# Reordering one stretch of the round in a two-stream transformer layer: where one stream's first scores run

## The chip, the cores and the metric

The kernel runs on one core of one Trainium2 chip. The metric is the device time of one execution in microseconds, taken as the median of several runs. Lower is better.

## What is computed

The first half of the reference is an attention block over eight sequences of 1024 rows of width 256. The second half, which the change concerns, takes that result `x` through two layers of local attention and a gated feed-forward network. Cut to what matters:

```python
h = shift_token(x)                     # second half of the width comes from the row before
q, k, v = split(h @ wqkv, 3)           # 8 heads of 64
q, k = l2norm(q) * qs, l2norm(k) * ks
q, k = rotary_xpos(q, k)
sim = q @ k.T                          # windows of 128 rows against 256 keys, masked
o = softmax(sim) @ v
x = x + o @ wo
h = layernorm(shift_token(x)) * lg + lb
a, g = split(h @ w1 + b1, 2)           # 682 each
x = x + (a * gelu(g)) @ w2 + b2
```

All of it is in float32.

## The kernel before

The eight sequences make two streams, X and Y, of four sequences each. A stream works through its sequences in tiles of 128 rows, and through both layers of a tile before the next tile: 4 sequences x 8 tiles x 2 layers = 64 units for each stream. Unit `n` of X and units `n` and `n-1` of Y share one round, so the rounds run over `n` (the helper `rounds`), and every engine has an order of its own for the steps of a round, written out by hand. A word such as `saX:0` is step `sa` of stream X for unit `n`; `woY:1` is step `wo` of stream Y for unit `n-1`. Each engine issues its steps strictly in the order of its string, and a step begins with waits on semaphores that the steps it depends on have raised. Streams have PSUM banks and buffers of their own (banks 0 to 3 for X, 4 to 7 for Y).

The steps of one unit, with the line in which each is issued and the engine:

- `uT` (TensorE, L792) transposes the input, `uTc` (VectorE, L1307 and L1310) takes it out; `ga`, `gb_`, `gb` (L799) and `v_`, `v` (L808) are the projections to q, k and v. Half `a` is heads 0 to 3, half `b` heads 4 to 7.
- `sqa`, `sqb` (ScalarE, L1001) square, `ssa`, `ssb` (VectorE, L1315) sum; `rk`, `rq` (GpSimd, L1541 and L1545) make the inverse norms. `rs`, `rot`, `ad` (VectorE, L1329, L1323, L1335) are the rotary products and their sum, and `kn` (VectorE, L1341) scales k by its norm.
- `tqa`, `tka`, `tqb`, `tkb` (TensorE, L820) transpose q and k of each half, two transposes a step. `qca`, `kca`, `qcb`, `kcb` (ScalarE, L1008, L1012) take them out; `vc` (ScalarE, L1005) takes v out. `qca` and `qcb` each wait for both transposing steps of their half.
- `sa`, `sb` (TensorE, L830) are the scores of four heads each. `m0`, `m1` (VectorE, L1353, then L1358) add mask and take the row maximum of them; `e0` to `e3` (ScalarE, L1019) are the exponentials of two heads each, `d0` to `d3` (VectorE, L1363, L1366) divide by the sums, `p0` to `p3` (TensorE, L838) transpose, and `pc0` to `pc3` (ScalarE, L1025) take out.
- `o` (TensorE, L847) is the product with v, `oc` (ScalarE, L1029) takes it out, `wo_`, `wo` (TensorE, L856) multiply by `wo`, `u1` (VectorE, L1370) adds the residual.
- `E` (L863, only where a tile has a tile before it in its sequence) and `sh` (L866) shift the rows on TensorE. `bnu`, `bns`, `ag` (VectorE, L1374, L1377, L1381), `rs` on GpSimd (L1549, L1552) and `hl` (VectorE, L1385) are the layer norm. `h` (TensorE, L871) transposes it, and `hT` (ScalarE, L1033) takes it out.
- `w10`, `w11`, `w12` (TensorE, L881) are the gate products, `ge0` to `ge2` (ScalarE, L1041) the gelu, `ac0` to `ac2` (VectorE, L1396) the product of gate and value, `w20` to `w22` (TensorE, L891) the last product, `ub` and `u2` (VectorE, L1389, L1402) the residual, `fin` and `ln` (VectorE, L1300, L1282) the end and the start of a tile.

Waits that the change touches, in the steps' own words:

```python
elif name in ("qca", "qcb"):
    act.wait_ge(w[f"s_t_ps{g}"], n * 2 + 2)
elif name in ("d0", "d1", "d2", "d3"):
    dve.wait_ge(w["s_exp"], n * 4 + m + 1)
elif name == "E":
    if t > 0:
        pe.wait_ge(w["s_pT"], n * 4 + 3)
elif name in ("w20", "w21", "w22"):
    pe.wait_ge(w["s_act"], n * FC + 2 * j + 2)
```

Of the kernel before, what the change touches and what calls it, by code (L numbers as in the profile page):

```python
# [66 lines left out]
def build(nc, x, Wa, ba, We, be, Wi, Wo, Wv, Wout, Wout_sw, head_vec, sgn, wqkv, q_scale, k_scale,  # L67
# [7 lines left out]
    with ctx:  # L75
# [186 lines left out]
        def rounds(order, do):  # L262

            steps = [(step[:-1], int(lag)) for step, lag in (word.split(":") for word in order.split())]
            names = [word.split(":")[0][-1] for word in order.split()]
            for n in range(-1, UNITS + 2):
                for (step, lag), name in zip(steps, names):
                    if 0 <= n - lag < UNITS:
                        do(step, X if name == "X" else Y, n - lag)
# [303 lines left out]
        def _(pe):  # L573
# [207 lines left out]
            def step_pe(name, w, n):  # L781
# [113 lines left out]
                else:  # L895
# [2 lines left out]
            pe.wait_ge(s_wf, 16 * loads[1])  # L898
            pe.wait_ge(s_zero, 5)
            rounds(("w10X:1 tqaY:1 w11X:1 tkaY:1 w12X:1 saY:1 w20X:1 tqbY:1 w21X:1 tkbY:1 w22X:1 uTX:0 sbY:1 gaX:0 p0Y:1 gb_X:0 "  # L900
                    "p1Y:1 gbX:0 v_X:0 p2Y:1 vX:0 p3Y:1 tqaX:0 tkaX:0 oY:1 saX:0 wo_Y:1 woY:1 tqbX:0 EY:1 shY:1 tkbX:0 sbX:0 hY:1 "
                    "p0X:0 w10Y:1 p1X:0 w11Y:1 p2X:0 w12Y:1 EX:0 w20Y:1 p3X:0 w21Y:1 oX:0 w22Y:1 wo_X:0 uTY:0 woX:0 gb_Y:0 shX:0 "
                    "gbY:0 gaY:0 hX:0 v_Y:0 vY:0"), step_pe)


# [1 line left out]
        def _(act):  # L907
# [87 lines left out]
            def step_act(name, w, n):  # L995
# [47 lines left out]
                else:  # L1043
# [2 lines left out]
            act.wait_ge(s_wf, 16 * loads[1])  # L1046
            act.wait_ge(s_zero, 5)
            rounds(("ge0X:1 ge1X:1 qcaY:1 kcaY:1 ge2X:1 e0Y:1 qcbY:1 kcbY:1 e1Y:1 sqaX:0 e2Y:1 e3Y:1 pc0Y:1 pc1Y:1 sqbX:0 pc2Y:1 "
                    "pc3Y:1 qcaX:0 vcX:0 kcaX:0 ocY:1 e0X:0 qcbX:0 kcbX:0 e1X:0 hTY:1 e2X:0 pc0X:0 e3X:0 pc1X:0 ge0Y:1 pc2X:0 "
                    "ge1Y:1 ge2Y:1 pc3X:0 ocX:0 sqbY:0 sqaY:0 hTX:0 vcY:0"), step_act)  # L1050


# [1 line left out]
        def _(dve):  # L1054
# [215 lines left out]
            def step_dve(name, w, n):  # L1270
# [132 lines left out]
                else:  # L1403
# [2 lines left out]
            dve.wait_ge(s_wf, 16 * loads[1])  # L1406
            dve.wait_ge(s_zero, 5)
            rounds(("rsbY:1 rotbY:1 adbY:1 ac0X:1 knbY:1 ac1X:1 ac2X:1 finY:2 m0Y:1 ubX:1 u2X:1 d0Y:1 uTcX:0 d1Y:1 m1Y:1 rsaX:0 "
                    "ssaX:0 d2Y:1 rotaX:0 d3Y:1 adaX:0 knaX:0 rotbX:0 ssbX:0 rsbX:0 adbX:0 m0X:0 u1Y:1 knbX:0 bnuY:1 bnsY:1 agY:1 "
                    "d0X:0 hlY:1 m1X:0 d1X:0 d2X:0 finX:1 d3X:0 lnY:0 ubY:1 ac0Y:1 ac1Y:1 leY:0 ac2Y:1 u2Y:1 uTcY:0 u1X:0 bnuX:0 "  # L1410
                    "lnX:-1 bnsX:0 agX:0 hlX:0 ssaY:0 rsaY:0 rotaY:0 adaY:0 knaY:0 leX:-1 ssbY:0"), step_dve)


# [201 lines left out]
```

## Time and profile before

| | |
|---|---|
| median of 3 runs | 5147.08 us (5144.16 to 5147.25) |
| profiled execution | 5151.58 us, of which the span is 5149.8 us |
| TensorE (PE) busy | 4820.2 us, 94% of the span |
| VectorE (DVE) busy | 3885.7 us, 75% |
| ScalarE (ACT) busy | 2876.1 us, 56% |
| GpSimd (POOL) busy | 1178.6 us, 23% |
| second half | from about 1950 us of the span to its end |

The engine names are those of the profile: PE is TensorE's matmuls and PEld its weight loads, DVE is VectorE, ACT is ScalarE, POOL is GpSimd. L-numbers are lines of the kernel. A timeline row gives the start in us, the duration in us, the engine, the line and operation, what it writes and reads, and how many instructions are merged in it; in brackets stands how long its engine was idle before it and what ended that. PEclk is the clock that TensorE was granted, as a share of full speed.

### The profile page before, as it was taken

The numbers are of one execution on the slowest core, as the hardware profiler recorded it, in microseconds if no ns is written. First come the engines' busy times: TensorE is split into PE (matmuls) and PEld (weight loads), VectorE is DVE, ScalarE is ACT, GpSimd is POOL, SyncE is SP. The second block draws the span as 40 slices with busy tenths as digits, with TensorE's granted clock in tenths as the row PEclk, the third lists the DMA queues.
The fourth block names the chain that finished last, engine by engine and source line by source line (L and its number), as shares of the span: only waits on it lengthen the run. The fifth ranks groups of instructions, "written<-read, shape, count | busy, mean of one in ns | idle before, by whom it ended". The sixth has DMA issues, their size and how long they took to land.

```text
span 5149.8 us, 85248 instructions
## 1 busy us (share of the span) xinstructions
PE 4820.2 (94%) x29996; PEld 2903.7 (56%) x29996; DVE 3885.7 (75%) x10911; ACT 2876.1 (56%) x6033; POOL 1178.6 (23%) x1722
## 2 busy tenths in 40 slices
PE   6799999999999997999999999999999999999998
PEld 2233333333333325777777777777777777777776
DVE  6688878788887865777777777777777777777776
ACT  1566666666666663555555555555555555555554
POOL 2202121121202002222222222222222222222222
PEclk7999999999999998999999999999999999999999
DMA  6333233233323311000000000000000000000000
GB/s 148 73 61 63 40 74 58 50 58 64 64 45 66 47 22 41 6 6 5 8 21 13 7 6 6 7 6 29 7 6 6 5 7 27 8 7 6 6 5 5
DMA packets 156588, 153.87 MB, mean 30 GB/s; under 512 B 25244, under 2 KB 148592, under 8 KB 156032
## 3 DMA queue, kind: packets, MB, share of 16 engines
q1 hardware_dynamic: 156160, 148.42, 14.1%
q8 instruction: 237, 3.88, 0.3%
q14 instruction: 191, 1.56, 0.1%
HBM read 103.49 MB, written 44.09 MB: 29 GB/s over the span
## 4 chain that ended last, share of the span: by engine, by line
PE 74%; DVE 12%; issue 4%; ACT 3%; DMA 2%; SPq 2%; POOL 2%; DVEq 0%; POOLq 0%; ACTq 0%
PE psum L881 13%; PE psum L645 8%; PE psum L663 7%; PE psum L799 7%; PE psum L675 6%; PE psum L891 5%; PE psum L847 5%; PE psum L808 4%; PE psum L838 4%; PE psum L830 3%; DVE big_s L1353 3%; DVE mx L1151 3%; PE psum L856 2%; PE psum L628 2%; PE psum L820 1%
## 5 line engine op out<-in xcount | busy, mean ns | idle before, releaser
L1151 DVE TENSOR_REDUCE mx<-psum 128x1 f32<-128x512 f32 x2048 | 1335.3, 687 | 302.0 <-PE psum L645 297.3
L955 ACT ACTIVATE pr<-psum 128x1024 f32<-128x1024 f32 x1024 | 1022.7, 1024 | 638.7 <-PE psum L663 627.5
L645 PE MATMUL psum<-stack 96*128 96x512 bf16 x2048 | 727.4, 389 | 63.3 <-DMA stack<-parts_d 21.5
L881 PE MATMUL psum<-hlT_s,w_sb 128*114 128x128 f32 (+1 forms) x6144 | 741.6, 274 | 30.0 <-ACT hlT_s L1033 30.0
L881 PEld LDWEIGHTS psum<-hlT_s,w_sb 128*114 128x114 f32 (+1 forms) x6144 | 702.9, 178 | 76.8 <-ACT hlT_s L1033 60.7
L1019 ACT ACTIVATE big_s<-big_s,mxl_s 128x256 f32<-128x256 f32 x1024 | 510.9, 502 | 301.5 <-DVE mxl_s L1358 301.5
L663 PE MATMUL psum<-stack 99*128 99x512 bf16 x2048 | 613.6, 381 | 22.7 <-DMA stack<-mrow 22.1
L645 PEld LDWEIGHTS psum<-stack 96*128 96x128 bf16 x2048 | 196.5, 96 | 749.8 <-DVE mx L1151 286.5
L1545 POOL TENSOR_TENSOR rn_s<-ss_s,neghalf 128x4 f32<-128x4 f32 x512 | 550.9, 1076 | 76.0
L675 PE MATMUL psum<-pr,vg 128*32 128x512 f32 x4096 | 546.7, 606 | 0.4 <-ACT pr L955 0.4
L799 PE MATMUL psum<-wqkv_sb,uT_s 128*128 128x512 f32 x1024 | 507.3, 608 | 0.7 <-DVE uT_s L1310 0.7
L1353 DVE CUSTOM_DVE_ANT_0 big_s<-psum,maskv,rn_s 128x256 f32<-128x256 f32 x1024 | 433.8, 482 | 66.6 <-PE psum L830 66.5
L1001 ACT ACTIVATE pT_s<-psum 128x512 f32<-128x512 f32 x256 | 152.4, 595 | 539.3 <-PE psum L799 539.3
L891 PE MATMUL psum<-w_sb,pT_s 114*128 114x256 f32 (+1 forms) x1536 | 408.1, 388 | 0.0
L1041 ACT ACTIVATE pT_s<-psum,b_sb 114x128 f32<-114x128 f32 (+1 forms) x768 | 238.8, 368 | 214.6 <-PE psum L881 213.9
L1541 POOL TENSOR_SCALAR ss_s<-ss_s 128x4 f32<-128x4 f32 x512 | 147.5, 288 | 922.2 <-DVE ss_s L1315 897.7
L1025 ACT ACTIVATE pT_s<-psum 128x512 f32<-128x512 f32 x512 | 294.4, 588 | 98.3 <-PE psum L838 98.3
L830 PE MATMUL psum<-kT_s,qT_s 64*128 64x256 f32 x2048 | 291.3, 403 | 61.4 <-ACT kT_s L1012 61.4
L838 PEld LDWEIGHTS psum<-ident,big_s 128*128 128x128 f32 x2048 | 250.1, 141 | 148.9 <-issue 102.3
L1366 DVE TENSOR_SCALAR big_s<-big_s,rz_s 128x256 f32<-128x256 f32 x1024 | 315.6, 351 | 18.5 <-DVE rz_s L1363 0.4
L1396 DVE SCALAR_TENSOR_TENSOR pT_s<-psum,b_sb,pT_s 114x128 f32<-114x128 f32 (+1 forms) x768 | 230.6, 346 | 113.9 <-ACT pT_s L1041 113.9
L838 PE MATMUL psum<-ident,big_s 128*128 128x128 f32 x2048 | 309.2, 274 | 6.9 <-DVE big_s L1366 6.8
(160 smaller groups left out, 6755.5 us busy)
## 6 DMA issues: line engine op xcount, KB each, us to landing
stack<-parts_d SPq DMA_DIRECT2D x384, 128.0 KB, 5.7
parts_d<-parts SPq DMA_DIRECT2D x64, 384.0 KB, 3.2
hn<-in_x SPq DMA_DIRECT2D x8, 1024.0 KB, 9.2
xr<-in_x SPq DMA_DIRECT2D x8, 1024.0 KB, 5.4
x_d<-xr SPq DMA_DIRECT2D x8, 1024.0 KB, 9.4
tab<-tab_d SPq DMA_DIRECT2D x32, 256.0 KB, 2.5
out_x<-o_s SPq DMA_DIRECT2D x64, 128.0 KB, 1.7
xs<-x_d SPq DMA_DIRECT2D x8, 896.0 KB, 7.5
```

What stands on the lines that cost most here:

```text
L645: pe.matmul(psum[:, to, :], stack[0:KS, g % 2, 0, u % 2, h, a * P:(a + 1) * P], stack[0:KS, g % 2, 1, kh, h, :], start=True, stop=True).th ...
L663: mm = pe.matmul(psum[:, h, :], stack[0:KS + PART, (u // 2) % 2, 1, kc // 4, h, (kc % 4) * P:(kc % 4 + 1) * P], stack[0:KS + PART, (u // 2 ...
L675: mm = pe.matmul(psum[h * VW:(h + 1) * VW, ACC, :], vg[:, (u // 2) % 2, kc, h, :], pr[:, e % 2, h, :], start=(kc == 0), stop=(kc == NT - 1))
L799: mm = pe.matmul(psum[:, bk + g, :], w["uT"][:, l, k * (P + 1):k * (P + 1) + P], wqkv_sb[:, l, k, 0:2 * INNER].rearrange("p (a g n) -> p g ...
L838: mm = pe.transpose(psum[:, bk + P_BANK[m], (2 * (h % 2) + kb) * P:(2 * (h % 2) + kb + 1) * P], w["big"][:, h, kb * P:(kb + 1) * P], ident[:])
L881: mm = pe.matmul(psum[0:rows, bk + G_BANK[j], m * P:(m + 1) * P], w1_sb[:, l, k, col:col + rows], w["hlT"][:, k, :], start=(k == 0), stop= ...
L891: mm = pe.matmul(psum[:, bk + 2, 0:D], hid[0:rows, cc, :], w2_sb[0:rows, l, cc, :], start=(cc == 0), stop=(cc == FC - 1))
L955: act.activation(pr[:, e % 2, 2 * pair:2 * pair + 2, :], psum[:, 2 * pair:2 * pair + 2, :], ACT.Exp, scale=DH ** -0.5).then_inc(s_exp, 1)
L1019: ins = act.activation(w["big"][:, h, :], w["big"][:, h, :], ACT.Exp, bias=w["mx"][:, h:h + 1], accum_out=w["z"][:, h:h + 1])
L1151: dve.tensor_reduce(mx[:, u % 2, m, kh:kh + 1], psum[:, src, :], AX.X, ALU.max).then_inc(s_max, 1)
L1353: ins = dve.tensor_tensor_reduce(out=w["big"][:, h, :], in0=psum[:, bk + at, col:col + 2 * P], in1=maskv[:, 0 if t == 0 else 2 - own], sca ...
L1545: gp.tensor_tensor(w["rn"][:, part], w["ss"][:, part], neghalf[:, 0:LH // 2], ALU.pow).then_inc(w[f"s_rn{g}"], 1)
```

## The change

Three order strings of the second half are edited; no instruction is added, removed or resized. On TensorE X's steps `tka` and `tqb` move behind and ahead of Y's `o` and `wo_` respectively, `tkb` moves ahead of Y's `E`, the first scores `sa` move from ahead of Y's `wo_` to behind Y's `sh`, next to `sb`, and `p0`, `p1`, `p2` of X each run one gate product of Y later. On ScalarE X's `e0` and `e1` move behind Y's `hT`. On VectorE X's `m0` moves from ahead of Y's `u1` to behind Y's `hl`, and `kn` of half `b` takes its place; `d0` moves behind it.

```diff
@@ step_pe
-  ... p3Y:1 tqaX:0 tkaX:0 oY:1 saX:0 wo_Y:1 woY:1 tqbX:0 EY:1 shY:1 tkbX:0 sbX:0 hY:1
-  p0X:0 w10Y:1 p1X:0 w11Y:1 p2X:0 w12Y:1 EX:0 w20Y:1 p3X:0 w21Y:1 oX:0 w22Y:1 wo_X:0 ...
+  ... p3Y:1 tqaX:0 oY:1 tkaX:0 tqbX:0 wo_Y:1 woY:1 tkbX:0 EY:1 shY:1 saX:0 sbX:0 hY:1
+  w10Y:1 p0X:0 w11Y:1 p1X:0 w12Y:1 p2X:0 EX:0 w20Y:1 p3X:0 w21Y:1 oX:0 w22Y:1 wo_X:0 ...
@@ step_act
-  ... pc3Y:1 qcaX:0 vcX:0 kcaX:0 ocY:1 e0X:0 qcbX:0 kcbX:0 e1X:0 hTY:1 e2X:0 pc0X:0 e3X:0 pc1X:0 ge0Y:1 pc2X:0
+  ... pc3Y:1 qcaX:0 vcX:0 kcaX:0 ocY:1 qcbX:0 kcbX:0 hTY:1 e0X:0 e1X:0 e2X:0 pc0X:0 e3X:0 pc1X:0 ge0Y:1 pc2X:0
@@ step_dve
-  ... rsbX:0 adbX:0 m0X:0 u1Y:1 knbX:0 bnuY:1 bnsY:1 agY:1
-  d0X:0 hlY:1 m1X:0 d1X:0 d2X:0 finX:1 d3X:0 lnY:0 ubY:1 ac0Y:1 ...
+  ... rsbX:0 adbX:0 knbX:0 u1Y:1 bnuY:1 bnsY:1 agY:1
+  hlY:1 m0X:0 d0X:0 m1X:0 d1X:0 d2X:0 finX:1 d3X:0 lnY:0 ubY:1 ac0Y:1 ...
```

## Rows read from the trace of the kernel before

**Rows 1.** The page's chain that ended last, shares of the span by engine.

```profile
PE 74%; DVE 12%; issue 4%; ACT 3%; DMA 2%; SPq 2%; POOL 2%; DVEq 0%; POOLq 0%; ACTq 0%
```

**Rows 2.** Busy time by stretch: us, PE, PEld, DVE, ACT, POOL, PEclk, DMA share, GB/s.

```profile
2012.00:5109.00 3097.00, 2928.06 (x20053) 2204.02 (x20053) 2296.84 (x7701) 1689.72 (x4640) 830.92 (x1380) 1.00 0.03 9
```

**Rows 3.** Timeline of one round around Y's `o`, and its `o` a round later.

```profile
3497.62 1.97 PE L847 MATMUL psum<-pT_s,v_s 128*64 128x128 f32 x32
3497.73 0.39 ACT L1008 ACTIVATE qT_s<-psum 128x256 f32<-128x256 f32 x1
3498.01 0.59 ACT L1005 ACTIVATE v_s<-psum 128x512 f32<-128x512 f32 x1
...
3498.49 0.39 ACT L1012 ACTIVATE kT_s<-psum 128x256 f32<-128x256 f32 x1
...
3499.09 0.69 DVE L1335 TENSOR_TENSOR big_s<-big_s 128x512 f32<-128x512 f32 x1
...
3499.63 0.60 ACT L1029 ACTIVATE oT_s<-psum 128x512 f32<-128x512 f32 x1 [0.76 <-PE psum L847]
...
3500.58 1.99 PE L856 MATMUL psum<-wo_sb,oT_s 128*128 128x256 f32 x8
...
3502.41 0.38 PE L820 MATMUL psum<-ident,big_s 128*128 128x128 f32 x2
...
3547.08 1.97 PE L847 MATMUL psum<-pT_s,v_s 128*64 128x128 f32 x32
```

**Rows 4.** Timeline, same round: from Y's residual to its gate products.

```profile
3502.61 0.42 DVE L1370 TENSOR_TENSOR u_s<-psum,u_s 128x256 f32<-128x256 f32 x1
...
3503.09 0.49 PE L866 MATMUL psum<-u_s,turned 128*128 128x128 f32 x2
...
3504.61 1.13 PE L830 MATMUL psum<-kT_s,qT_s 64*128 64x256 f32 x8 [0.75 <-ACT kT_s L1012]
...
3505.43 0.35 DVE L1385 TENSOR_SCALAR hl_s<-u_s,mv_s,rs_s 128x128 f32<-128x128 f32 x1 [0.52 <-POOL rs_s L1552]
...
3506.16 0.44 PE L871 MATMUL psum<-ident,hl_s 128*128 128x128 f32 x2 [0.41 <-DVE hl_s L1385]
...
3506.63 0.81 ACT L1033 ACTIVATE hlT_s<-psum,lnv 128x128 f32<-128x128 f32 x2 [1.10 <-PE psum L871]
...
3507.49 2.00 PE L881 MATMUL psum<-hlT_s,w_sb 128*114 128x128 f32 x16 [0.46 <-ACT hlT_s L1033]
```

**Rows 5.** Timeline, earlier in that round: stream Y's `m0`, `d0` and X's `uTc`.

```profile
3485.33 0.48 DVE L1353 CUSTOM_DVE_ANT_0 big_s<-psum,maskv,rn_s 128x256 f32<-128x256 f32 x1
...
3488.40 0.17 DVE L1363 RECIPROCAL rz_s<-z_s 128x2 f32<-128x2 f32 x1 [0.31 <-ACT big_s L1019]
...
3489.13 0.15 DVE L1307 COPY uT_s<-uT_s 128x1 f32<-128x1 f32 x1
```

**Rows 6.** Timeline, the same round as 3 and 4: `m1X` to `w20Y`.

```profile
3506.01 0.48 DVE L1353 CUSTOM_DVE_ANT_0 big_s<-psum,maskv,rn_s 128x256 f32<-128x256 f32 x1
...
3511.02 1.28 ACT L1041 ACT_TABLE_LOAD   x1
...
3512.83 0.60 ACT L1025 ACTIVATE pT_s<-psum 128x512 f32<-128x512 f32 x1
3512.98 0.61 DVE L1396 SCALAR_TENSOR_TENSOR pT_s<-psum,b_sb,pT_s 114x128 f32<-114x128 f32 x2 [1.27 <-ACT pT_s L1041]
...
3513.70 0.39 PE L863 MATMUL psum<-u_s,wrap 128*128 128x128 f32 x2
...
3513.92 1.03 PE L891 MATMUL psum<-w_sb,pT_s 114*128 114x256 f32 x4
```

**Rows 7.** Timeline of TensorE in the last round, where only stream Y is left.

```profile
5122.88 0.66 PE L838 MATMUL psum<-ident,big_s 128*128 128x128 f32 x4 [3.14 <-DVE big_s L1366]
5123.87 1.12 PE L838 MATMUL psum<-ident,big_s 128*128 128x128 f32 x4 [0.33 <-DVE big_s L1366]
5124.91 3.10 PE L847 MATMUL psum<-pT_s,v_s 128*64 128x128 f32 x32
```

**Rows 8.** Busy time of a stretch in that last round, columns as in 2.

```profile
5124.00:5126.00 2.00, 2.00 (x14) 1.67 (x16) 0.00 (x0) 1.00 (x2) 0.00 (x0) 0.50 0.04 8
```

More of the change, by code:

```diff
@@ L900, in _ @@
             rounds(("w10X:1 tqaY:1 w11X:1 tkaY:1 w12X:1 saY:1 w20X:1 tqbY:1 w21X:1 tkbY:1 w22X:1 uTX:0 sbY:1 gaX:0 p0Y:1 gb_X:0 "
-                    "p1Y:1 gbX:0 v_X:0 p2Y:1 vX:0 p3Y:1 tqaX:0 tkaX:0 oY:1 saX:0 wo_Y:1 woY:1 tqbX:0 EY:1 shY:1 tkbX:0 sbX:0 hY:1 "
-                    "p0X:0 w10Y:1 p1X:0 w11Y:1 p2X:0 w12Y:1 EX:0 w20Y:1 p3X:0 w21Y:1 oX:0 w22Y:1 wo_X:0 uTY:0 woX:0 gb_Y:0 shX:0 "
+                    "p1Y:1 gbX:0 v_X:0 p2Y:1 vX:0 p3Y:1 tqaX:0 oY:1 tkaX:0 tqbX:0 wo_Y:1 woY:1 tkbX:0 EY:1 shY:1 saX:0 sbX:0 hY:1 "
+                    "w10Y:1 p0X:0 w11Y:1 p1X:0 w12Y:1 p2X:0 EX:0 w20Y:1 p3X:0 w21Y:1 oX:0 w22Y:1 wo_X:0 uTY:0 woX:0 gb_Y:0 shX:0 "
                     "gbY:0 gaY:0 hX:0 v_Y:0 vY:0"), step_pe)
@@ L1048, in _ @@
             rounds(("ge0X:1 ge1X:1 qcaY:1 kcaY:1 ge2X:1 e0Y:1 qcbY:1 kcbY:1 e1Y:1 sqaX:0 e2Y:1 e3Y:1 pc0Y:1 pc1Y:1 sqbX:0 pc2Y:1 "
-                    "pc3Y:1 qcaX:0 vcX:0 kcaX:0 ocY:1 e0X:0 qcbX:0 kcbX:0 e1X:0 hTY:1 e2X:0 pc0X:0 e3X:0 pc1X:0 ge0Y:1 pc2X:0 "
+                    "pc3Y:1 qcaX:0 vcX:0 kcaX:0 ocY:1 qcbX:0 kcbX:0 hTY:1 e0X:0 e1X:0 e2X:0 pc0X:0 e3X:0 pc1X:0 ge0Y:1 pc2X:0 "
                     "ge1Y:1 ge2Y:1 pc3X:0 ocX:0 sqbY:0 sqaY:0 hTX:0 vcY:0"), step_act)
@@ L1408, in _ @@
             rounds(("rsbY:1 rotbY:1 adbY:1 ac0X:1 knbY:1 ac1X:1 ac2X:1 finY:2 m0Y:1 ubX:1 u2X:1 d0Y:1 uTcX:0 d1Y:1 m1Y:1 rsaX:0 "
-                    "ssaX:0 d2Y:1 rotaX:0 d3Y:1 adaX:0 knaX:0 rotbX:0 ssbX:0 rsbX:0 adbX:0 m0X:0 u1Y:1 knbX:0 bnuY:1 bnsY:1 agY:1 "
-                    "d0X:0 hlY:1 m1X:0 d1X:0 d2X:0 finX:1 d3X:0 lnY:0 ubY:1 ac0Y:1 ac1Y:1 leY:0 ac2Y:1 u2Y:1 uTcY:0 u1X:0 bnuX:0 "
+                    "ssaX:0 d2Y:1 rotaX:0 d3Y:1 adaX:0 knaX:0 rotbX:0 ssbX:0 rsbX:0 adbX:0 knbX:0 u1Y:1 bnuY:1 bnsY:1 agY:1 "
+                    "hlY:1 m0X:0 d0X:0 m1X:0 d1X:0 d2X:0 finX:1 d3X:0 lnY:0 ubY:1 ac0Y:1 ac1Y:1 leY:0 ac2Y:1 u2Y:1 uTcY:0 u1X:0 bnuX:0 "
                     "lnX:-1 bnsX:0 agX:0 hlX:0 ssaY:0 rsaY:0 rotaY:0 adaY:0 knaY:0 leX:-1 ssbY:0"), step_dve)
```

## Prediction

> **What bounds the kernel now.** I read the page's chain first: three quarters of it is PE [rows 1]. Then the busy time of the second half: over its 3097 us PE is busy for 2928, DVE for 2297, ACT for 1690, at a granted clock of 1.00 [rows 2]. So the engine that is to be kept fed is PE, and what counts is any stretch in which it must wait. A round is 49.46 us long, the distance of Y's `o` from the next one [rows 3], and 64 units fit in the second half, so 1 us in a round is worth about 63 us.
>
> Then I read the timeline of one round in detail, because an order is an argument about who stands behind whom, and totals don't show that. The reader is to see two things. First, the chain from Y's `wo` through residual, shift, norm and transpose to `w10Y` is a latency chain over four engines, and PE waits in it three times: 0.75 us ahead of `sbX`, 0.41 ahead of `hY`, 0.46 ahead of `w10Y` [rows 4]. Second, from `w10Y` on PE doesn't wait for anything until the last products of the unit: `EX` and `w20Y` follow at 3513.70 and 3513.92, and the product that `w20Y` needs (`ac0Y`) was ready at 3512.98 + 0.61 = 3513.59, the probabilities that `EX` needs (`pc2X`) at 3512.83 + 0.60 = 3513.43 [rows 6]. So those two inputs arrive only 0.3 us before they are used. What makes them late has no slack to give.
>
> **Part 1: `tkaX` behind `oY`.** ACT's `qcaX` waits for both transposing steps of its half, so it now waits for `tkaX`, which waits its turn behind the 32 matmuls of `oY`. Queued behind `qcaX` on ACT are `vcX`, `kcaX` and then `ocY`, and PE's `wo_Y` waits for `ocY`. Before, the first three ran while `oY` ran and `ocY` started 0.04 us after its end [rows 3]. Now: `oY` starts two transposes earlier, which I put at 0.2 us (estimate from 0.38 for a pair, whose ends overlap what follows), at 3497.4; it ends at 3497.4 + 1.97 = 3499.4; `tkaX` behind it takes 0.38, so with the overlap `qcaX` starts at about 3499.7. From `qcaX` to `vcX` is 0.28, from `vcX` to `kcaX` 0.48, and from `kcaX` to its successor 0.28 as behind the like-sized `qcaX`: `ocY` starts at 3500.75 and ends 0.60 later at 3501.35, and `wo_Y` starts at 3501.4, where it started at 3500.58 [rows 3]. That is +0.83 us. `tqbX` runs in that wait (its input, `adbX`, is there at 3499.09 + 0.69 = 3499.78). From both sides: if PE's queue hides nothing of `tkaX`, +0.95; if `oY` starts no earlier and the transposes overlap fully, +0.6.
>
> **Part 2: `m0X` away from `u1Y`.** It looks as if `m0X` held `u1Y` up, but `u1Y` started at 3502.61 and `woY` ended at 3500.58 + 1.99 = 3502.57 [rows 3, 4]: nothing is gained. `knbX` no longer stands behind `u1Y`, but `bnsY` waited for `shY` (3503.09 + 0.49 = 3503.58), not for `knbX`. `tkbX` is earlier against `woY` and `sbX` no longer waits 0.75, but `hY` is set by the norm: its input comes at a fixed distance from `woY`, so the time goes over into the wait ahead of `hY`. So `hlY` moves by the 0.83 of part 1 from 3505.43 to 3506.26, and `w10Y` from 3507.49 to 3508.32 [rows 4].
>
> **Part 3: `m0X`, `e0X`, `d0X`, `m1X` in a row on DVE.** This is the main term. Before, `m0X`, `e0X`, `e1X` and `d0X` ran ahead of `hlY`, under the norm's latency, and `m1X` followed `hlY` at once, at 3506.01, 0.58 after `hlY`'s start [rows 4, 6]. Now `m0X` stands in that place, at 3506.84, and `d0X` right behind it waits for `e0X`, which waits for `m0X`. Behind `d0X` on DVE are `m1X`, `d1X`, `d2X`, `finX`, `d3X`, `ubY` and `ac0Y`. What this costs the trace shows for the other stream: Y's `m0` to the first instruction of `d0` is 3488.40 - 3485.33 = 3.07, and from there to the next step on DVE 0.73 [rows 5]. So `m1X` starts at 3506.84 + 3.07 + 0.73 = 3510.64, 4.63 later than before.
>
> Everything from `m1X` to `w20Y` keeps its order: `e2X`, `pc0X`, `e3X`, `pc1X`, the table load, `ge0Y`, `pc2X` on ACT, `ac0Y` on DVE. `m1X` to the table load was 5.01, to `pc2X` 6.82, to `ac0Y` 6.97 [rows 6]. The new places: load 3515.65, `pc2X` 3517.46 to 3518.06, `ac0Y` 3517.61 to 3518.22. `EX` starts at 3518.1 and `w20Y` 0.22 behind it, at 3518.3, where it was 3513.92: +4.4 us. The slack of 0.3 is in this. PE alone would have got there at 3508.32 + (3513.92 - 3507.49) + at most 0.66 for `p0X`, whose cover (the wait ahead of `w10Y`) is gone [rows 4, 6, 7], that is by 3515.4. So ACT and DVE decide, and PE stands idle for some 2 us ahead of `EX`, besides about 0.9 ahead of `hY`, 0.9 ahead of `w10Y` and 0.6 ahead of `p0X` (which needs `d0X`, ready near 3510.7).
>
> Is the loss given back later in the round? From `w20Y` on the order is as before, every step hangs on PE's, and PE waited for little there. I see no slack, so the whole 4.4 stays. No DMA, and no step of GpSimd or of SyncE's queue, changes its place; their work hangs on steps that only get later. With both bounds of part 1 and 0.2 for the spacings that I took from like steps, it is 4.0 to 4.7 us a round.
>
> **Sum.** The change bites in rounds that hold both streams: 63 of 65; the first has only X and the last only Y. 63 x 4.4 = 277 us. On the profiled execution, 5151.6 (its span 5149.8), that gives 5429; the median of the runs stands 4.5 lower, so 5147 + 277 = 5424, and with a little for rounds whose tile has no tile before it (no `EX`, where `w20Y` was 0.2 earlier before) 5425.
>
> **Rivals.**
> - *The clock falls as well.* At the end, where PE had been idle for 3.14 us and again for 0.33, the granted clock went to 0.50, which is 1.2 GHz of 2.4 [rows 7, 8]; a set of four transposes took 1.12 instead of 0.66 and `o` 3.10 instead of 1.97 [rows 3, 7]. One such fall in each round costs 0.46 + 1.13 = 1.6 us, at most 63 x 1.6 = 100 us: 5525. For it: the idle time would gather between `hY` and `w20Y`. Against it: the longest wait that I work out is 2.2 us, shorter than that one, and 0.5 to 1 us waits in rounds of today leave the clock at 1.00. The Trainium skill ("TensorE: Matmul & The Clock Gate", section "Why this matters for your kernels") warns of throughput drops from idle gaps between bursts of matmuls; by that rule this rival would be the likely one if the gaps came near the length of the one in the last round.
> - *Only PE's own terms count.* If DVE and ACT got from `hlY` to `ac0Y` in time after all, +0.83 and the uncovered `p0X` at 0.44 to 0.66 remain: about 1.3 us a round, 82 us: 5229. Against it is that DVE can't start `m1X` while `d0X` waits.
> - *Faster.* The three waits that I named sum to 1.62 us a round. If scores side by side and `knbX` ahead of `u1Y` won all of them, and the chain behind `m1X` came no more than 0.3 us later than today, the kernel would be 63 x 1.62 = 102 us faster: 5045. It decides if `m1X` could start by 3506.3, which would need `e0X` done before `hlY`; the order forbids it.
> - *No effect*, within 0.2%: only if PE had slack of 4 us somewhere in the round, which a busy share of 2928 in 3097 leaves no room for [rows 2].
>
> **How the numbers follow.** Chances: the forecast 0.72, with its own range 5385 to 5455; the clock 0.13 (mostly a part of its price, 5455 to 5525); PE's own terms or some giving back in between 0.10 (5200 to 5385); faster 0.03; no effect 0.02. The range reaches from 5370 to 5490: what it leaves out is most of the middle rival, the two on the other side, and the upper end of the clock. A change of less than 0.2% can't be told from none. Slower by more than that are the first three, 0.95.
>
> **What would show it.** In the new timeline: `ocY` (L1029) about 1 us after the end of `oY` (L847), and a PE wait ahead of L856 released by ACT; DVE idle for 1.1 to 1.2 us ahead of an L1363, with L1353 of `m1X` some 4.4 us behind L1385; PE idle some 2 us ahead of L863 or L891, ended by ACT or DVE; a round near 53.9 us; PEclk still 1.00 and PE's share in the second half near 87%. I would be wrong if `m1X` were not late, if ACT put the load ahead of `e3X`'s end, or if the later part of the round shrank against today's.

## The result and the profile after

The changed kernel takes 5479.0 us (median of 4 runs, 5476.9 to 5481.3) against 5147.2 before: a ratio of 1.064 (95% interval 1.063 to 1.066), 332 us slower. The forecast was 5425 with a range of 5370 to 5490.

The page's chain and busy time after, to be read against [rows 1]:

```profile
PE 4919.4 (90%) x29996; PEld 2951.1 (54%) x29996; DVE 3901.7 (71%) x10911; ACT 2868.2 (52%) x6033; POOL 1171.9 (21%) x1722
...
PE 64%; DVE 15%; ACT 11%; issue 4%; DMA 2%; SPq 2%; POOL 2%; POOLq 0%; DVEq 0%; ACTq 0%
```

The instruction counts are the same, and ACT now holds 11% of the chain where it held 3%. TensorE's busy time grew by 99 us although it got no more work. Some of that comes with more waiting alone: `m1_first` below waits nearly as much, its clock never falls, and its busy time is 31 us above that of the kernel before. The rest is another matter. The second half by stretch, with the columns of [rows 2], shows a clock that is no longer whole:

```profile
2012.00:5430.00 3418.00, 3019.39 (x20006) 2247.00 (x20005) 2307.01 (x7682) 1677.71 (x4627) 819.50 (x1373) 0.98 0.03 8
```

The timeline of one round after, from Y's `o` to `wo_Y`, answers to [rows 3]:

```profile
3544.05 0.38 PE L820 MATMUL psum<-ident,big_s 128*128 128x128 f32 x2
...
3544.36 1.97 PE L847 MATMUL psum<-pT_s,v_s 128*64 128x128 f32 x32
...
3546.26 0.44 PE L820 MATMUL psum<-ident,big_s 128*128 128x128 f32 x2
3546.74 0.38 ACT L1008 ACTIVATE qT_s<-psum 128x256 f32<-128x256 f32 x1 [1.88 <-PE psum L820]
...
3547.76 0.62 ACT L1029 ACTIVATE oT_s<-psum 128x512 f32<-128x512 f32 x1
3548.43 1.99 PE L856 MATMUL psum<-wo_sb,oT_s 128*128 128x256 f32 x8 [1.13 <-ACT oT_s L1029]
```

ScalarE stood idle for 1.88 us ahead of `qcaX`, which waited for `tkaX`, and TensorE waited 1.13 us for `ocY` behind it. From `oY` to `wo_Y` it is 4.07 us, where it was 2.96.

The same round from `hlY` to `w20Y` answers to [rows 4, 6]:

```profile
3553.74 0.47 DVE L1353 CUSTOM_DVE_ANT_0 big_s<-psum,maskv,rn_s 128x256 f32<-128x256 f32 x1
3553.88 0.44 PE L871 MATMUL psum<-ident,hl_s 128*128 128x128 f32 x2 [0.53 <-DVE hl_s L1385]
...
3555.22 2.00 PE L881 MATMUL psum<-hlT_s,w_sb 128*114 128x128 f32 x16 [0.90 <-ACT hlT_s L1033]
...
3556.80 0.17 DVE L1363 RECIPROCAL rz_s<-z_s 128x2 f32<-128x2 f32 x1 [1.16 <-ACT big_s L1019]
...
3557.54 0.48 DVE L1353 CUSTOM_DVE_ANT_0 big_s<-psum,maskv,rn_s 128x256 f32<-128x256 f32 x1
...
3557.68 0.66 PE L838 MATMUL psum<-ident,big_s 128*128 128x128 f32 x4 [0.46 <-DVE big_s L1366]
...
3562.53 1.28 ACT L1041 ACT_TABLE_LOAD   x1
...
3564.34 0.60 ACT L1025 ACTIVATE pT_s<-psum 128x512 f32<-128x512 f32 x1
3564.49 0.61 DVE L1396 SCALAR_TENSOR_TENSOR pT_s<-psum,b_sb,pT_s 114x128 f32<-114x128 f32 x2 [1.27 <-ACT pT_s L1041]
```

The fence above ends with `ac0Y`; what TensorE does then:

```profile
3564.99 0.49 PE L863 MATMUL psum<-u_s,wrap 128*128 128x128 f32 x2 [1.95 <-ACT pT_s L1025]
3565.32 1.03 PE L891 MATMUL psum<-w_sb,pT_s 114*128 114x256 f32 x4
```

`m0X` to `d0X` is 3.06 us, `d0X` to `m1X` 0.74, DVE idle for 1.16 of it. `EX` stands 1.95 us for `pc2X`.

In this round the clock stayed whole. In the round before it, the same place looked like this:

```profile
3509.47 0.49 PE L863 MATMUL psum<-u_s,wrap 128*128 128x128 f32 x2 [1.94 <-ACT pT_s L1025]
...
3509.80 1.57 PE L891 MATMUL psum<-w_sb,pT_s 114*128 114x256 f32 x4
...
3511.16 1.06 PE L838 MATMUL psum<-ident,big_s 128*128 128x128 f32 x4
...
3512.01 1.79 PE L891 MATMUL psum<-w_sb,pT_s 114*128 114x256 f32 x4
```

The three steps behind `EX` take 1.57, 1.06 and 1.79 instead of 1.03, 0.60 and 1.03. The stretches of 4 us behind the two waits, columns as in [rows 2]:

```profile
3509.50:3513.50 4.00, 4.00 (x14) 3.13 (x14) 2.37 (x8) 1.55 (x5) 0.00 (x0) 0.58 0.00 0
3565.00:3569.00 4.00, 4.00 (x40) 3.46 (x42) 1.22 (x5) 1.57 (x5) 0.00 (x0) 1.00 0.00 0
```

In the first, TensorE was granted 0.58 on the mean, that is, mostly its lower level of 1.2 GHz, and got 14 matmuls done; in the second 1.00 and 40 (26 of them the short ones of `oX`). The trace's record of the granted clock has 33 such falls between 2020 us and 5430 us, all behind this wait (four of them in rounds without an `EX`, behind one of 2.10 ahead of `w20Y`); the kernel before has none there.

Take the distance from one `ocY` to the next as a round. The 30 undisturbed rounds last 53.83 us on the mean and the 33 others 55.31, against 49.39 before. These means don't give the price of a fall, because the two groups hold different rounds: those in which X ends a tile are 0.15 us shorter and have most of the falls, and the last, in which only Y is left, is shorter still. The run `fill3` below has the same order and no fall in this place, so it can be compared round by round. A round without a fall lasts the same in both, to 0.02 us. Each of 32 rounds with a fall is longer in the changed kernel, by 1.68 us on the mean (1.61 to 1.70). The 63 rounds of `fill3`, with two falls elsewhere, take 276 us more than those of the kernel before, 4.38 a round. So the order costs 276 us and the falls 32 x 1.68 = 54, together 330 of the 332.

### The profile page after: what moved, and what is told of

Its sections match the earlier page's. It is cut to its first block, busy times and chain, and to the rows that moved or that the text cites. A ratio compares the mean times of both kernels' runs of the same rounds, so it can differ in the third digit from the quotient of the medians.

```text
span 5478.5 us, 85248 instructions
## 1 busy us (share of the span) xinstructions
PE 4919.4 (90%) x29996; PEld 2951.1 (54%) x29996; DVE 3901.7 (71%) x10911; ACT 2868.2 (52%) x6033; POOL 1171.9 (21%) x1722
## 4 chain that ended last, share of the span: by engine, by line
PE 64%; DVE 15%; ACT 11%; issue 4%; DMA 2%; SPq 2%; POOL 2%; POOLq 0%; DVEq 0%; ACTq 0%
PE psum L645 7%; PE psum L663 6%; PE psum L799 6%; PE psum L881 6%; PE psum L675 6%; PE psum L891 6%; DVE big_s L1353 5%; PE psum L847 4%; ACT big_s L1019 4%; PE psum L856 4%; PE psum L808 4%; DVE mx L1151 3%; PE psum L838 3%; PE psum L830 2%; PE psum L628 2%
## 5 line engine op out<-in xcount | busy, mean ns | idle before, releaser
L891 PE MATMUL psum<-w_sb,pT_s 114*128 114x256 f32 (+1 forms) x1536 | 450.2, 419 | 14.7 <-DVE pT_s L1396 14.7
L838 PE MATMUL psum<-ident,big_s 128*128 128x128 f32 x2048 | 331.8, 287 | 45.1 <-DVE big_s L1366 36.5
L891 PEld LDWEIGHTS psum<-w_sb,pT_s 114*128 114x128 f32 (+1 forms) x1536 | 286.8, 207 | 75.5 <-DVE pT_s L1396 26.6
L856 PE MATMUL psum<-wo_sb,oT_s 128*128 128x256 f32 x1024 | 259.3, 386 | 72.9 <-ACT oT_s L1029 72.9
```

The lines of the kernel that those rows point to most:

```text
L838: mm = pe.transpose(psum[:, bk + P_BANK[m], (2 * (h % 2) + kb) * P:(2 * (h % 2) + kb + 1) * P], w["big"][:, h, kb * P:(kb + 1) * P], ident[:])
L891: mm = pe.matmul(psum[:, bk + 2, 0:D], hid[0:rows, cc, :], w2_sb[0:rows, l, cc, :], start=(cc == 0), stop=(cc == FC - 1))
```

## The experiments

**One round's arithmetic for all.** Below, "undisturbed" is the mean round with no fall of the clock in it, without the first and the last round. The kernel before ran again beside each group, and the ratios are against those runs: 5148.7 us beside `fill5`, `tka_back`, `row_only` and `m1_first`, 5152.3 beside `p1_ac0`, 5151.6 beside the others. So two medians of different groups can differ by some 4 us without meaning anything.

| kernel | median us | ratio (95%) | undisturbed round | falls |
|---|---|---|---|---|
| before | 5147.2 | 1 | 49.39 | 0 |
| changed | 5479.0 | 1.064 (1.063 to 1.066) | 53.83 | 33 |
| `fill5` | 5455.6 | 1.060 (1.058 to 1.061) | 54.22 | 1 |
| `fill3` | 5425.8 | 1.053 (1.052 to 1.055) | 53.74 | 2 |
| `tka_back` | 5431.0 | 1.055 (1.054 to 1.057) | 52.69 | 47 |
| `row_only` | 5383.5 | 1.046 (1.044 to 1.047) | 52.96 | 27 |
| `m1_first` | 5378.9 | 1.045 (1.043 to 1.047) | 53.04 | 0 |
| `both_undone` | 5315.1 | 1.032 (1.030 to 1.033) | 51.90 | 1 |
| `pe_only_p1` | 5264.8 | 1.022 (1.021 to 1.024) | 50.51 | 25 |
| `p1_early` | 5132.7 | 0.997 (0.995 to 0.998) | 49.11 | 0 |
| `p1_ac0` | 5127.9 | 0.995 (0.994 to 0.997) | 49.03 | 0 |

**Is it the clock? More work in the wait (`fill5`).**

```diff
-                    for h in (2 * m, 2 * m + 1):
+                    for h in (2 * m, 2 * m + 1) * (5 if m == 2 and w is X else 1):
                         for kb in range(2):
                             mm = pe.transpose(psum[:, bk + P_BANK[m], ...
```

> The changed kernel, but X's third set of probability transposes (p2X) is issued five times over instead of once, ahead of the wait in front of EX; the result is the same, 4 x 0.44 = 1.76 us of matmuls are added to each round, into the stretch in which TensorE was idle for 1.95 us. Theory A (the 55 us above the worked-out 277 are the falls of the granted clock to 0.50 that follow this wait, in about half the rounds): the falls vanish, the rest stays, about 5424 us, so the kernel gets faster with more work in it. Rival B (the 55 us are waits further on in the round, or the count of transposes costs time): 5479 or up to 110 us more, if the added work isn't hidden.

Measured: 5455.6 us, and all falls but one are gone. So the falls do follow the idle stretch, but the kernel gained 23 us, not 55: its rounds last 54.2, 0.4 more than the undisturbed rounds of the changed kernel. The one that is left lies elsewhere, ahead of `p0X`. Half a verdict, since `pc2X` waits for the last of these transposes: four more sets were too many.

**The same with less filling (`fill3`).** The factor is 3 in place of 5.

> As fill5, with p2X's transposes issued three times instead of five: 2 x 0.44 = 0.88 us more matmuls a round. In fill5 the rounds took 54.2 us against 53.8 in the undisturbed rounds of the changed kernel: the last transposes ended about 0.4 us too late for pc2X. Here they end in time, and the wait ahead of EX is 1.07 us long, about that of m1_first (0.9), in which the clock never fell. Theory A (a fall costs 1.5 us, and the wait of 1.95 us brings it about): 53.8 in every round, no falls, 5427 us. Rival B (what fill5 gained came from elsewhere): 5455 or more.

Measured: 5425.8 us. TensorE in one round, where the added transposes are merged with `p2X`'s own (12 in place of 4):

```profile
3537.45 1.47 PE L838 MATMUL psum<-ident,big_s 128*128 128x128 f32 x12
3539.98 0.49 PE L863 MATMUL psum<-u_s,wrap 128*128 128x128 f32 x2 [1.06 <-ACT pT_s L1025]
3540.31 1.03 PE L891 MATMUL psum<-w_sb,pT_s 114*128 114x256 f32 x4
3541.17 0.60 PE L838 MATMUL psum<-ident,big_s 128*128 128x128 f32 x4
```

`EX` starts when it did, only its wait is 1.06 instead of 1.95, and what follows runs at full speed. A kernel with 512 more matmuls is 53 us faster (58 when each is set against the runs of the kernel before beside it): the 54 us of the falls. None is left behind the wait ahead of `EX`; the two in the table lie ahead of `p0X`. Since the rounds without a fall last the same in both kernels, this isolates the clock from the order; the order's 276 us remain.

**Part 1 undone (`tka_back`).**

```diff
-  tqaX:0 oY:1 tkaX:0 tqbX:0 wo_Y:1
+  tqaX:0 tkaX:0 oY:1 tqbX:0 wo_Y:1
```

> The changed kernel with one edit undone: tkaX runs ahead of oY again, so that qcaX, vcX and kcaX on ScalarE are done before ocY. Theory A (part 1 of the prediction): wo_Y follows oY after 2.7 us instead of 4.07, and the round gets shorter by 1.1 us; the order of DVE is as in the changed kernel, so its cost and the falls of the clock stay: 5479 - 63 x 1.1 = 5409 us. Rival B (the wait for ocY is covered by the later waits ahead of hY and EX, which sit on a chain of their own): 5479.

Measured: 5431.0 us, 48 less rather than 70. In its timeline `ocY` again starts at once, and `wo_Y` 2.67 us after `oY`:

```profile
3520.02 1.97 PE L847 MATMUL psum<-pT_s,v_s 128*64 128x128 f32 x32
...
3522.04 0.60 ACT L1029 ACTIVATE oT_s<-psum 128x512 f32<-128x512 f32 x1 [0.76 <-PE psum L847]
```

Its undisturbed rounds are 1.14 us shorter, as worked out (1.1). What is missing of the 70 us went to the clock, which fell 47 times instead of 33 although the wait ahead of `EX` is as long: 14 more falls at 1.6 us are 22 us. So tkaX's place does cost what theory A says, and how many rounds a wait of 1.9 us disturbs is not fixed by its length alone.

**TensorE's order of before under the new DVE order (`row_only`).** Against the changed kernel TensorE has `tkaX` ahead of `oY`, `saX` ahead of `wo_Y` and `tkbX` behind `shY` again:

```diff
-  tqaX:0 oY:1 tkaX:0 tqbX:0 wo_Y:1 woY:1 tkbX:0 EY:1 shY:1 saX:0 sbX:0 hY:1
+  tqaX:0 tkaX:0 oY:1 saX:0 wo_Y:1 woY:1 tqbX:0 EY:1 shY:1 tkbX:0 sbX:0 hY:1
```

> TensorE's order of the kernel before (tkaX ahead of oY, saX ahead of wo_Y, tkbX behind shY) but with p0X to p2X one gate product later, and the ScalarE and VectorE orders of the changed kernel (e0X, e1X behind hTY; m0X, d0X, m1X in a row behind hlY). Theory A (part 3 carries most of the loss whatever TensorE does): m1X 3.80 us later than before, less 0.3 of slack, plus 0.2 for EX behind pc2X: 5147 + 63 x 3.7 = 5380, and 55 more for the same wait ahead of EX with its falls of the clock: 5435 us. Rival B (the loss comes from moving the scores and transposes on TensorE, so it is gone here): 5147 to 5200.

Measured: 5383.5 us. Its undisturbed rounds last 52.96, which is 3.57 more than before, where 3.7 were worked out. That is 225 us, four fifths of the 276, with the scores on TensorE where they had been. Rival B is out. The expectation was 52 too high mainly because I put the falls in at 55 us. 27 came, but only 7 lie behind the wait ahead of `EX`, where each costs 1.6 to 1.8 us. The 20 others begin in the wait ahead of `w10Y` or at its end, behind waits of 0.75 and 0.35 us, as here:

```profile
4412.87 1.13 PE L830 MATMUL psum<-kT_s,qT_s 64*128 64x256 f32 x8 [0.75 <-ACT kT_s L1012]
4414.36 0.44 PE L871 MATMUL psum<-ident,hl_s 128*128 128x128 f32 x2 [0.35 <-DVE hl_s L1385]
4415.69 3.55 PE L881 MATMUL psum<-hlT_s,w_sb 128*114 128x128 f32 x16 [0.90 <-ACT hlT_s L1033]
...
4425.46 0.49 PE L863 MATMUL psum<-u_s,wrap 128*128 128x128 f32 x2 [1.41 <-ACT pT_s L1025]
```

The granted clock in two of those microseconds, columns as in [rows 2]:

```profile
4416.00:4418.00 2.00, 2.00 (x11) 2.00 (x11) 0.81 (x4) 1.85 (x7) 0.00 (x0) 0.50 0.00 0
```

`w10Y` takes 3.55 us at the lower clock where it took 2.00, but the wait ahead of `EX` shrinks from 1.94 to 1.41 and takes the delay up. Such a round is no longer than an undisturbed one, within 0.1 us, in 19 of these 20. So a fall is paid for only where no wait stands behind it, and no single long wait is needed to bring one about.

**One swap in the row (`m1_first`).**

```diff
-  hlY:1 m0X:0 d0X:0 m1X:0 d1X:0
+  hlY:1 m0X:0 m1X:0 d0X:0 d1X:0
```

> The changed kernel with one swap on VectorE: m1X ahead of d0X, so that DVE doesn't wait for e0X before the second maxima. Theory A: m1X starts about 2 us earlier, but p0X then waits for d0X behind m1X (1.2 us on TensorE ahead of w11Y) and pc0X with it; the table load comes about 0.85 us earlier and the wait ahead of EX shrinks to about 1 us: 5479 - 54 = 5425, and with the falls of the clock gone 5370. Rival B (the cost is the row as a whole, every member of which must run before ge0Y, so the order inside it doesn't matter): 5479.

Measured: 5378.9 us, 100 less than the changed kernel by swapping two steps of DVE. TensorE and ACT in one round:

```profile
3511.03 0.66 PE L838 MATMUL psum<-ident,big_s 128*128 128x128 f32 x4 [1.08 <-DVE big_s L1366]
...
3514.52 1.28 ACT L1041 ACT_TABLE_LOAD   x1
...
3516.98 0.49 PE L863 MATMUL psum<-u_s,wrap 128*128 128x128 f32 x2 [0.93 <-ACT pT_s L1025]
```

The wait ahead of `EX` is 0.93, part of it has become one of 1.08 ahead of `p0X`, and the clock doesn't fall. Rounds of the same kind are 0.73 us shorter than the undisturbed ones of the changed kernel, where 0.85 had been worked out. So half of the 100 us is order (46 us), half clock (54).

**Both (`both_undone`).** The edits of `tka_back` and `m1_first` together.

> The changed kernel with tkaX ahead of oY again and m1X ahead of d0X. Theory A (the two terms add, since tkaX sets where hlY stands and the swap sets how long hlY to w20Y takes): 53.04 (the round of m1_first) - 1.14 (tka_back against the changed kernel's undisturbed rounds) = 51.9 us a round, no falls of the clock: 5147 + 63 x 2.5 = 5305. Rival B (one hides behind the other): 5379.

Measured: 5315.1 us, undisturbed rounds 51.90. The two add. It is still 3.2% slower than before, 2.5 us a round. What is left of the change is `m0X`, `e0X` and `e1X` behind `hlY`, the later scores, and `p0X` to `p2X` one gate product later. How the 2.5 us divide among these no run shows; the row is the likely one, as argued in part 3.

**Using what was learnt (`p1_early`, `pe_only_p1`), from the kernel before.**

```diff
@@ step_pe   (pe_only_p1: this line alone)
-  p0X:0 w10Y:1 p1X:0 w11Y:1 p2X:0
+  p0X:0 p1X:0 w10Y:1 w11Y:1 p2X:0
@@ step_act
-  hTY:1 e2X:0 pc0X:0 e3X:0 pc1X:0 ge0Y:1
+  hTY:1 pc0X:0 pc1X:0 e2X:0 e3X:0 ge0Y:1
@@ step_dve
-  hlY:1 m1X:0 d1X:0 d2X:0
+  hlY:1 d1X:0 m1X:0 d2X:0
```

> From the kernel before, not the changed one. d1X on VectorE goes ahead of m1X, p1X on TensorE goes from behind w10Y to ahead of it, next to p0X, and pc0X and pc1X on ScalarE go ahead of e2X, into the time in which ScalarE waits for m1X. The theory that came out of the change (what stands between hlY and ac0Y on DVE and ACT has 0.3 us of slack; TensorE has 0.6 us of waiting ahead of w10Y): p1X's 0.44 us of matmuls move into the wait ahead of w10Y; m1X comes 0.73 later, the two take-outs save 1.08 ahead of the table load, so the load comes 0.35 earlier and nothing new waits: 5147 - 64 x 0.44 = 5119 us. Rival (anything put ahead of m1X comes out as lost time at w20Y, as in the changed kernel): 5147 + 63 x 0.45 = 5175.

> The kernel before with TensorE's part of p1_early alone: p1X ahead of w10Y, DVE and ACT as before, so that d1X stays behind m1X. Theory: w10Y now waits behind p1X for d1X at 3508.64, 1.2 us after hlT was ready; TensorE loses 1.2 + 0.44 - 0.44 us a round up to w11Y: 5147 + 63 x 1.2 = 5223. Rival (the order on TensorE alone makes the gain): 5119.

Measured: `p1_early` 5132.7 us, 0.35% faster than before (ratio 0.9965, 0.9953 to 0.9978), `pe_only_p1` 5264.8. The second lost 1.12 us in its undisturbed rounds, as worked out (1.2), and another 40 us to 25 falls of the clock, which begin late in a wait of 1.7 us ahead of `p1X` or right behind it. The expectation had left these out. In `p1_early`, from `hY` on:

```profile
3545.00 0.44 PE L871 MATMUL psum<-ident,hl_s 128*128 128x128 f32 x2 [0.40 <-DVE hl_s L1385]
...
3545.28 1.10 PE L838 MATMUL psum<-ident,big_s 128*128 128x128 f32 x8
...
3546.34 3.75 PE L881 MATMUL psum<-hlT_s,w_sb 128*114 128x128 f32 x32
...
3549.61 1.28 ACT L1041 ACT_TABLE_LOAD   x1
...
3552.49 1.13 PE L891 MATMUL psum<-w_sb,pT_s 114*128 114x256 f32 x4 [0.22 <-DVE pT_s L1396]
```

`p0X` and `p1X` (8 transposes) fill the wait ahead of `w10Y`, whose row has no idle time any more. The table load comes 3.27 us after `w10Y`'s start, where it came 3.53 after [rows 4, 6]. The gain is 0.3 and not 0.44 us a round, and the last row says where some of it went: here `w20Y` waits 0.22 for `ac0Y`, which in this kind of round, where X ends a tile, has `finX`, `lnY` and `ubY` ahead of it on DVE. Rounds of this kind gained 0.17 us, the others 0.37.

**The last wait (`p1_ac0`).** From `p1_early`, on DVE `ac0Y` ahead of `ubY`.

> p1_early with ac0Y ahead of ubY on VectorE. In p1_early's trace the rounds in which X ends a tile and Y starts one (finX, lnY on DVE) gained 0.2 us, the others 0.4: w20Y waited 0.22 us for ac0Y, which stood behind lnY and ubY. Theory: both kinds of round gain 0.4: p1_early less 32 x 0.2 = 6 us, about 0.5% faster than the kernel before. Rival (w20Y's wait is hidden by a later one): as p1_early, 0.35% faster.

Measured: 5127.9 us, 0.46% faster than the kernel before (ratio 0.9954, 0.9940 to 0.9967). Against `p1_early` it is 5 us less, with intervals that overlap. The traces say more: the rounds in which X ends a tile went from 49.13 to 48.95 us, the others stayed at 49.1, as the expectation has it. It is the fastest version of this study and beats both kernels.

## Why the prediction was right, step by step

- **Part 1** (`wo_Y` +0.83): measured, against `oY`'s start, 4.07 - 2.96 = 1.11, less the 0.28 by which `oY` starts earlier behind `tqaX` (0.31 us after its start at 3544.05, where it was 0.59), so +0.83. In the undisturbed rounds, undoing it alone is worth 1.14 (`tka_back`). The row of before for this:

```profile
3497.03 0.66 PE L820 MATMUL psum<-ident,big_s 128*128 128x128 f32 x4
```

- **Part 2** (nothing gained by freeing `u1Y`; `sbX`'s wait goes over into `hY`'s): the wait ahead of `sbX` is gone and the one ahead of `w10Y` grew from 0.46 to 0.90, with `p0X` no longer in it. `hY` waits 0.53, where I had put 0.9.
- **Part 3** (3.07 + 0.73 from `m0X` to `m1X`): 3.06 + 0.74. Stream Y's own `m0`, `e0`, `d0` had given the price to a hundredth. `m1X` to the load is 4.99 (5.01), to `ac0Y` 6.95 (6.97).
- **The wait ahead of `EX`** (about 2 us): 1.95. **The round** (near 53.9): 53.83. Next to nothing was given back later: the sum of 277 us for the order measured as 276, by the rounds of `fill3`, which has the order without the falls. That its median, 5425.8, meets the forecast of 5425 is partly chance, since the kernel before ran 4.5 us slower beside it than beside the changed one: it is 274 us above its own runs of before, where 278 were forecast.
- **The clock** was where it failed. The 5479 us lie above the forecast's own range of 5385 to 5455, in the stretch that was left to the clock with a chance of 0.13. The step that failed is the sentence "the longest wait that I work out is 2.2 us, shorter than that one", with "PEclk still 1.00" behind it: I kept the fall out of the likeliest case because that wait was shorter than the 3.14 us of the last round. A fall followed the wait ahead of `EX` or `w20Y`, 1.95 or 2.10 us long, in 33 of 63 rounds. The rival's price for each fall, taken from that last round, was 1.6 us and measured 1.7. So its price was right and its condition wrong, and the time lay between the two cases, inside the range. That it lay inside is luck: nothing in the prediction said that only half of the rounds would fall, and with a fall in each the same figures give 5147 + 276 + 63 x 1.68 = 5529, above the range's 5490. The rule of the Trainium skill that I set beside it ("TensorE: Matmul & The Clock Gate", section "Why this matters for your kernels": avoid idle gaps between bursts of matmuls) named the right mechanism. But the gaps that it warns of are longer than the 1.95 us that were enough here, and the measurement decides.
- **The other rivals:** the gain of back-to-back scores didn't come. The wait ahead of `sbX` is gone, but it belonged to a latency chain that starts at `oY`, and the waits further down that chain grew: from 0.41 to 0.53 us ahead of `hY`, from 0.46 to 0.90 ahead of `w10Y`.

## What to carry to other kernels

On engines that run in order, price a moved step by the distance from where its row can now start to the first instruction of another engine that needs the row's end; the sum of the steps' durations says nothing, and the same three steps for the other stream often show the distance ready-made. Before filling one engine's wait, measure the slack of what stands behind it on the other engines (here 0.3 us, against 3.8 us put in); a fill that also takes work off that path, as `p1_early` does, wins. And count an idle stretch of TensorE twice: once for itself, once for the matmuls behind it if the granted clock falls, unless a later wait takes that second part up.

## What the runs showed of the hardware

- In the changed kernel the granted clock fell to 0.50 behind a TensorE wait of 1.95 us (2.10 where a round has no `EX`) in 33 rounds of 63. With 1.06 us (`fill3`, 1.22 without an `EX`) or 0.93 (`m1_first`, 1.1) at the same place it never fell there. Where nothing behind it took the delay up, a fall cost 1.7 us. Repeated transposes put into the wait made the kernel 53 us faster.
- The longest wait is not the measure. In `row_only` 20 of 27 falls began behind waits of 0.75 and some 0.35 us and in one of 0.90 or at its end, and 19 of those cost nothing. The few falls of `fill5`, `fill3` and `both_undone` lie in that part of the round too, around waits of 0.8 to 1.2 us ahead of `hY` and 0.90 ahead of `w10Y`. The kernel before has 0.75, 0.41 and 0.46 there and no fall, and `m1_first` has 1.17 and 0.90 in the round where `fill3` falls behind 1.16 and 0.90, and no fall either.
- Which rounds fall is not settled by the wait alone: the same 1.9 us gave 33 falls with rounds of 53.8 us, mostly in every second round, and 46 (of 47 in all) with rounds of 52.7. The runs don't show what picks them; that stays open.
